# Attention by four heads at a time, values in a rotation of five PSUM banks, and a new plan of the step

## What is computed

```python
qg = split_heads(tokens @ Wqg, HEADS)          # tokens: layer norm of x
kv = split_heads(tokens @ Wkv, HEADS)
queries, gates = (qg[..., :DIM_KEYS], qg[..., DIM_KEYS:])
keys, values = (kv[..., :DIM_KEYS], kv[..., DIM_KEYS:])
queries, keys, values = (l2norm(queries), l2norm(keys), l2norm(values))
sim = jnp.einsum('bhid,bhjd->bhij', queries, keys)
attn = jnp.square(jax.nn.relu(sim))
aggr = jnp.einsum('bhij,bhjd->bhid', attn, values)
out = tanh_norm(aggr) * jnp.tanh(jax.nn.silu(gates))
x = x + out.reshape(b, n, h * d) @ Wout
...
topk_idx, topk_weight = _gate(h, gate_kernel, gate_bias)   # h: layer norm of the new x
g = jnp.einsum('nh,ehm->enm', h, w_gate)
u = jnp.einsum('nh,ehm->enm', h, w_up)
inter = jax.nn.silu(g) * u
y = jnp.einsum('ne,enh->nh', combine, jnp.einsum('enm,emh->enh', inter, w_down))
shared = jnp.dot(jax.nn.silu(jnp.dot(h, sw_gate)) * jnp.dot(h, sw_up), sw_down)
x = x + y + shared
```

## Time and profile before

| | |
|---|---|
| three runs | 689.94 us median (686.68 to 690.36) |
| profiled execution | 687.0 us, span 685.3 us |
| TensorE (PE) busy | 646.5 us, 94% of the span, 5048 matmuls |
| weight loads (PEld) | 501.7 us, 73% |
| VectorE, ScalarE, GpSimd busy | 446.9, 427.7, 420.2 us (65, 62, 61%) |
| granted TensorE clock, mean | 0.998 |
| DMA moved | 76.14 MB, queue q1 69.2% of 16 engines' span |
| L572, values on TensorE | 1024 matmuls, 145.5 us busy, 9.4 us idle before them |
| L389, squares on GpSimd | 256, 260.9 us busy, 1040 ns each |

### The profile page before, as it was taken

How to read it: one execution, slowest core, us unless ns; L and a number is a source line. 1 busy time by engine, 2 the same in 40 slices (tenths; PEclk the granted TensorE clock), 3 DMA queues, 4 the chain that set the end, 5 groups by cost and what they waited for, 6 DMA issues and landing times.

```text
span 685.3 us, 15157 instructions
## 1 busy us (share of the span) xinstructions
PE 646.5 (94%) x5048; PEld 501.7 (73%) x5048; DVE 446.9 (65%) x1701; ACT 427.7 (62%) x986; POOL 420.2 (61%) x424
## 2 busy tenths in 40 slices
PE   2788998999999999999999999999999999999877
PEld 2555566777777778777778777878778787767777
DVE  5473647676766757576676767576675766555585
ACT  3578675666677675666776675666867566544312
POOL 3157855766757576776758585776768585686300
PEclk9999999999999999999999999999999999999999
DMA  9989949496784949497694949597694939503000
GB/s 253 142 136 150 118 102 114 103 139 108 131 135 102 107 132 122 88 154 117 121 134 109 112 131 112 98 148 124 115 131 101 121 102 124 101 5 76 9 1 16
DMA packets 75517, 76.14 MB, mean 111 GB/s; under 512 B 9296, under 2 KB 73392, under 8 KB 73648
## 3 DMA queue, kind: packets, MB, share of 16 engines
q1 hardware_dynamic: 75440, 75.17, 69.2%
HBM read 56.05 MB, written 19.10 MB: 110 GB/s over the span
## 4 chain that ended last, share of the span: by engine, by line
PE 84%; DVE 5%; ACT 5%; issue 3%; POOL 2%; DMA 1%; SPq 0%; DVEq 0%; ACTq 0%; POOLq 0%
PE ps_a L572 18%; PE ps_f L421 13%; PE ps_f L422 10%; PE ps_f L423 10%; PE ps_f L488 9%; PE ps_f L512 9%; PE ps_s L540 7%; PE ps_f L463 3%; PE ps_f L484 3%; POOL p L389 2%; PE ps_f L468 1%; PE ps_f L497 1%; DMA big<-in_L_attn_Wkv 1%; ACT r L678 1%; ACT sq L638 1%
## 5 line engine op out<-in xcount | busy, mean ns | idle before, releaser
L389 POOL TENSOR_TENSOR p<-r 128x512 f32<-128x512 f32 x256 | 260.9, 1040 | 177.5 <-ACT r L678 108.9
L572 PE MATMUL ps_a<-p,v 128*64 128x256 f32 x1024 | 145.5, 394 | 9.4 <-DVE big L994 4.7
L678 ACT ACTIVATE r<-ps_s 128x512 f32<-128x512 f32 x256 | 140.7, 613 | 13.5 <-PE ps_s L540 10.6
L994 DVE TENSOR_TENSOR big<-ps_a,big 128x256 f32<-128x256 f32 x128 | 54.1, 423 | 77.8 <-ACT big L687 77.2
L572 PEld LDWEIGHTS ps_a<-p,v 128*64 128x64 f32 x1024 | 64.4, 136 | 50.1 <-DVE big L994 7.7
L670 ACT ACTIVATE it<-ps_f 128x256 f32<-128x256 f32 x144 | 56.2, 390 | 49.4 <-PE ps_f L423 41.8
L408 POOL TENSOR_TENSOR it<-it,cb 128x512 f32<-128x512 f32 x56 | 71.2, 1282 | 18.9 <-DMA cb<-c_rows 18.8
L644 ACT ACTIVATE big<-ps_f 128x512 f32<-128x512 f32 x64 | 38.2, 598 | 66.2 <-PE ps_f L423 66.2
L949 DVE TENSOR_TENSOR it<-ps_f,it 128x256 f32<-128x256 f32 x144 | 60.6, 421 | 27.7 <-ACT it L670 26.5
L512 PE MATMUL ps_f<-wdown,it 128*128 128x128 f32 x576 | 70.4, 277 | 0.8 <-DVE it L966 0.8
L512 PEld LDWEIGHTS ps_f<-wdown,it 128*128 128x128 f32 x576 | 67.6, 192 | 2.4 <-DVE it L949 1.0
(11 more groups left out here) (159 smaller groups left out, 1430.1 us busy)
## 6 DMA issues: line engine op xcount, KB each, us to landing
qk_rows<-qk_parts SPq DMA_DIRECT2D x16, 1024.0 KB, 4.8
qkt<-qk_rows SPq DMA_DIRECT2D x64, 256.0 KB, 9.9
qkt<-qk_rows SPq DMA_DIRECT2D x128, 128.0 KB, 9.0
cb<-c_rows SPq DMA_DIRECT2D x28, 512.0 KB, 6.0
x_in<-in_L_attn_tokens SPq DMA_DIRECT2D x16, 128.0 KB, 6.3
x_res<-in_L_attn_tokens SPq DMA_DIRECT2D x16, 128.0 KB, 8.7
out<-o_sb SPq DMA_DIRECT2D x16, 128.0 KB, 8.6
big<-in_L_attn_Wqg SPq DMA_DIRECT2D x1, 640.0 KB, 4.5
```

What stands on the lines that cost most here:

```text
L389: pool.tensor_tensor(p[h % 4][:], r[h % 2][:], r[h % 2][:], ALU.mult).then_inc(probs_done, 1)
L572: last = pe.matmul(ps_a[64 * e:64 * e + 64, 0:N], v[s % 3][:, t, h * DV:(h + 1) * DV], p[h % 4][:, t * N:(t + 1) * N], start=(t == 0), sto ...
L678: act.activation(r[h % 2][:], ps_s[h % 2][:], ACT.Relu).then_inc(relu_done, 1)
```

## The change

FILL is written anew, with values as a job ("A", "av", j) of its own, two at a time, in slots 1, 3, 5 and 7. The jobs use five banks ps_f0 to ps_f4 in turn; ps_a and its semaphores go. TensorE does scores j+2, values j, values j+1, scores j+3, all pairs counted on into the next step. ScalarE squares and VectorE multiplies two pairs at a time, in slots 0, 2, 4 and 6. GpSimd's and VectorE's orders are new: the routing is done in one piece in slot 0 (route_experts was in slot 2), cD comes in slot 1 (it was in slot 3), the root of L's variance in slot 3, L408 in slots 3, 5 and 7. SP's order is unchanged.

```diff
-        [("F", "lg", 0), ("P", "v", 3), ("D", "y2", 0), ("N", "ones", 0)],
-        [("N", "nT", 0), ("D", "y2", 1), ("P", "g", 0)],
-        [("F", "gu", 0), ("F", "gu", 1), ("P", "g", 1), ("F", "gu", 2)],
-        [("F", "gu", 3), ("F", "cD", 0), ("P", "g", 2), ("O", "rT", 0), ("F", "gu", 4)],
-        [("O", "rB", 0), ("O", "rB", 1), ("F", "gu", 5), ("O", "rB", 2), ("L", "xT", 0), ("O", "rB", 3), ("P", "g", 3)],
-        [("O", "y", 0), ("O", "y", 1), ("L", "qk", 0)],
-        [("F", "gu", 6), ("L", "qk", 1), ("L", "v", 0), ("F", "gu", 7)],
-        [("L", "v", 1), ("F", "gu", 8), ("O", "x2T", 0), ("L", "v", 2), SKIP, SKIP],
+        [("F", "lg", 0), ("P", "g", 0), ("D", "y2", 0), ("P", "v", 3), ("N", "ones", 0)],
+        [("D", "y2", 1), ("N", "nT", 0), ("F", "cD", 0), ("P", "g", 1), ("A", "av", 0), ("A", "av", 1)],
+        [("F", "gu", 0), ("P", "g", 2), ("F", "gu", 1), ("F", "gu", 2)],
+        [("F", "gu", 3), ("F", "gu", 4), ("F", "gu", 5), ("O", "rT", 0), SKIP, ("A", "av", 2), ("A", "av", 3)],
+        [("O", "rB", 0), ("O", "rB", 1), ("L", "xT", 0), ("O", "rB", 2), ("O", "rB", 3), ("P", "g", 3), ("L", "qk", 0)],
+        [("O", "y", 0), ("L", "qk", 1), ("L", "v", 0), ("O", "y", 1), SKIP, ("A", "av", 4), ("A", "av", 5)],
+        [("F", "gu", 6), ("L", "v", 1), ("F", "gu", 7)],
+        [("F", "gu", 8), ("O", "x2T", 0), SKIP, ("L", "v", 2), ("A", "av", 6), ("A", "av", 7)],
...
-            bank.update({job[1:]: ps_f[n % 4] for n, job in enumerate(order(s)) if job != SKIP})
+            bank.update({job[1:]: ps_f[n % 5] for n, job in enumerate(order(s)) if job != SKIP})
...
 # GpSimd, step
+                    if k == 6 and "O" in on:
+                        pool.wait_ge(ch_n, 3 * s)
+                        root(rstd2, var2, rstd2_ready)
                     if "A" in on:
                         for h in (2 * k, 2 * k + 1):
-                            wait(pool, values_done, 8 * s + (h - 4) // 2 + 1)
+                            wait(pool, done["av"], 8 * s + (h - 4) // 2 + 1)
...
-                    if k == 1 and "L" in on:
+                    if k == (1 if at == FIRST_STEP else 3) and "L" in on:
...
-                    if "P" in on and k == 4:
-                        scale_values(s + 1, 0, (0, 1))
...
-                    if "F" in on and at < B and k in (5, 6, 7):
-                        b = s - 2
-                        for j in ((0, 1), (2,), (3,))[k - 5]:
...
+                    if "P" in on and k in (4, 5):
+                        scale_values(s + 1, 0, (k - 4,))
+                    if "F" in on and at < B:
+                        for j in {3: (0, 1), 5: (2,), 7: (3,)}.get(k, ()):
+                            scale_by_combine(s - 2, j)
...
 # TensorE, step
+                            if kind == "av" and j % 2 == 0:
+                                scores_ahead(s, q, j + 2)
                             wait_for_bank(n, s, at)
                             filler(stage, kind, j, s, q, on, at)
+                            if kind == "av" and j % 2 == 1:
+                                scores_ahead(s, q, j + 2)
...
-                    if k < SLOTS - 1:
-                        if "A" in on:
-                            scores(s, q, k + 1)
-                    elif "A" in stages(at + 1):
-                        scores(s + 1, 1 - q, 0)
-                    if "A" in on:
-                        wait(pe, aw_done, 8 * s + k)
...
 # ScalarE, step
+                for k in range(SLOTS):
+                    if k % 2 == 0:
+                        relu(k)
+                        if ("A" in on and k > 0) or ("O" in on and k == 0):
+                            squared_heads(k)
+                    else:
+                        relu(k)
...
+                        if (kind, j) in gates_behind and "P" in on:
+                            gates(gates_behind[(kind, j)], s, q)
```

More of the change, by code:

```diff
@@ L73, in order @@
         return [job for slot in fill(s) for job in slot]
-    assert all(len(plan) == SLOTS and sum(len(slot) for slot in plan) % 4 == 0 for plan in (FILL, *ENDS.values()))
+    assert all(len(plan) == SLOTS and sum(len(slot) for slot in plan) % 5 == 0 for plan in (FILL, *ENDS.values()))
     OFFSET = {"L": 2, "P": 1, "N": 1, "A": 0, "O": -1, "F": -2, "D": -3}
     JOBS = {"xT": 1, "qk": 2, "v": 4, "g": 4, "ones": 1, "nT": 1, "rT": 1, "rB": 4, "y": 2,
-            "x2T": 1, "lg": 1, "gu": FC, "cD": 1, "cT": 1, "cB": 4, "y2": 2}
+            "x2T": 1, "lg": 1, "gu": FC, "av": NP, "cD": 1, "cT": 1, "cB": 4, "y2": 2}
     BY_DMA = B - 2
@@ L544, in scores, with scores_ahead, values @@
                             last.then_inc(scores_done, 1)
+            def scores_ahead(s, q, k):
+                if k < NP:
+                    scores(s, q, k)
+                elif "A" in stages(s + 1):
+                    scores(s + 1, 1 - q, k - NP)
+            def values(b, k, ps):
+                if k in (0, 4):
+                    pe.wait_ge(v_normed, 4 * b + (2 if k == 0 else 4))
+                for t in range(T):
+                    for e in range(2):
+                        h = 2 * k + e
+                        if t == 0:
+                            pe.wait_ge(probs_done, 16 * b + h + 1)
+                        last = pe.matmul(ps[64 * e:64 * e + 64, 0:N],
+                                         v[b % 3][:, t, h * DV:(h + 1) * DV], p[h % 4][:, t * N:(t + 1) * N],
+                                         start=(t == 0), stop=(t == T - 1))
+                return last
             def step(s, q, on, at):
@@ L672, in step, with relu @@
             def step(s, q, on, at):
-                for k in range(SLOTS):
+                def relu(pair):
                     if "A" in on:
-                        for h in (2 * k, 2 * k + 1):
+                        for h in (2 * pair, 2 * pair + 1):
                             wait(act, probs_done, 16 * s + h - 1)
@@ L678, in step, with squared_heads @@
                             act.activation(r[h % 2][:], ps_s[h % 2][:], ACT.Relu).then_inc(relu_done, 1)
-                    if ("A" in on and k > 0) or ("O" in on and k == 0):
-                        pair, b = (k - 1, s) if k > 0 else (NP - 1, s - 1)
+                def squared_heads(k):
+                    for i in range(2):
+                        pair, b = (k - 2 + i, s) if k > 0 else (NP - 2 + i, s - 1)
                         if pair == 0:
@@ L685, in step @@
                                 act.wait_ge(w_lo, 4)
[L686 to L687 removed]
+                        ps = (bank if k > 0 else bank_before)[("av", pair)]
+                        act.wait_ge(done["av"], NP * b + pair + 1)
+                        act.activation(a2[:, pair, :], ps[:, 0:N], ACT.Square).then_inc(a2_done, 1)
+                for k in range(SLOTS):
[5 more added lines that the diff above has]
+                        relu(k)
                     if at == -1 and k == 4:
```

147 lines of the change are left out of this document (64 added, 83 removed).

## The result

The changed kernel takes **709.32 us** (median of 4 runs, 705.82 to 714.17) beside 689.25 us of the kernel before on the same chip: a ratio of 1.031, with the 95% interval 1.0254 to 1.0365. It is 3% slower. The profiled execution took 712.05 us, its span is 710.3 us against 685.3, and 5048 matmuls are 5048 as before. The steps, from nT to nT, tell where the 25.0 us went: the first three take 3.1 us more than before, the twelve in the middle 21.9 more (mean 40.86 against 39.04), the last two 2.1 less, and 2.1 lie before the first nT and behind the last, about half in each. So it is a loss of every step with the combine weights in it.

A forecast was written before the change was run, and what follows sets the result against it. A ring from GpSimd's scaling through low_parts(1) and DMA, 40.4 us a step against 38.86, was to bound: 687.0 + 18.5 - 1.4 = 704.1, put at 705 us. Own range 697 to 712; 8 in 10, 676 to 712.

The forecast's parts named there:

- The ring: GpSimd's scaling of `it` through low_parts(1) and DMA to the next scaling: 7.4 + 33.0, 40.4 us a step (39.7 to 41.1).
- The sum: Twelve ring periods add 18.5 us, the last two steps give back 1.4: 687.0 to 704.1, forecast put at 705.
- The start: First two steps, without scaling by combine weights: TensorE waits for starts, counted as nothing, between -3 and +2 us.
- Where TensorE waits: TensorE idles 2 to 3 us a step, before values of pair 4 or 5 (GpSimd's square) and scores 6 (Relu).
- Banks: PSUM banks, every fifth job now read: found read in time, pair 3 within tenths; cost 0 to 0.3 us, taken as 0.
- What the switches save: Fewer changes of matmul form on TensorE save 1.2 us a step; TensorE alone needs 37.7, 0.4 more if score exits are free.
- Pair 3: Pair 3's values wait for gate_up(4) to free a bank: 0 to 0.3 us a step, taken as 0.
- head 15: Last head's values wait for p behind Silu, Relu and squares: about 0.5 us a step, if nothing else stops TensorE first.
- Rival 1: Small write c_rows overtakes the loads, ring 36.3 us, switches decide: 677 us, or 668 with the 0.5 hidden; chance 0.20.
- Rival 2: Emptying PSUM takes what the switches give, 1.2 us a step: about the same time, 688 us; chance 0.14.
- Rival 3: Ring binds harder: TensorE idles 2 to 3 us a step, its granted clock falls; kept inside the forecast (0.66), towards 712.
- Weight loads as the measure of TensorE: Skill's metric: weight loads 31.10 of 40, a fifth free, fewer form changes worth nothing; the prediction went by gaps instead.

The follow-up runs named there:

- experiments 1: Changed kernel with only part 0 of the scaling of `it` in GpSimd's slot 3, part 1 moved to slot 5 with part 2; 699.76 us, ratio 1.0174.
- 2: Changed kernel with parts 0, 1 and 2 of the scaling of `it` all in GpSimd's slot 3; 728.06 us, ratio 1.0576.
- experiment 3: Changed kernel with the scaling of `it` back in the slots of the kernel before (5, 6, 7); 682.1 us, ratio 0.9926.
- 10: Changed kernel with scaling in slots 4, 5, 7, first two steps' statistics earlier, and gate_up(4) ahead of value_scales; 678.03 us, ratio 0.9847.
- experiment 4: Changed kernel with the two Relus of pair 5 behind the copy and square of qk1 on ScalarE, scaling still in slot 3; 693.55 us, ratio 1.0087.
- 9: Changed kernel with only six of the twelve q and k loads from the third batch on, so the output differs; 678.64 us, ratio 0.9854.
- Experiment 12: Version 10 plus, on ScalarE, pair 7's Relus before gu 7's Silu and next batch's first Relu before v 2's copy and square; 675.73 us, ratio 0.9834.
- Experiment 8: Changed kernel with c_rows and cb issued from ScalarE's queue in place of SP's; 724.91 us, ratio 1.0553.
- experiment 5: As experiment 3, with the first two steps' layer norm sums and root two slots earlier; 679.4 us, ratio 0.9893.

## Why the prediction was right

- **The ring**, the step on which the forecast stood, held in each of its parts. L388 to the end of low_parts(1): 7.33 to 7.37 us in all twelve periods, predicted 7.4. From there to the next L388: 32.2 to 34.3, mean 33.25, predicted 33.0 and at most 33.7 on average. Ring: 40.62 by the thirteen starts of L388, predicted 40.4. It moved as it should in experiments 1 and 2, and was gone when opened at GpSimd (3, 10), in part at ScalarE (4), and at the DMA (9).
- **The sum.** Of 18.5 us for the twelve steps it was 21.9. Of the 3.4 that are missing, 2.6 is the ring's 0.22 us, twelve times over; the rest is the first of the twelve, 43.93 us beside 40.85 before. The last two steps gave back 2.1 (predicted 1.4). The start, predicted between -3 and +2, cost 3.1 in its first three steps and 1.0 before the first nT: it missed its range. Behind the last nT there is another 1.0, for which the sum has no term. The median of 709.32 is 4 us above the forecast, and that flatters the sum. The terms were added to the profiled execution, 687.0 to 704.1, and the profiled execution was 712.05: 8 us short. The medians lie closer because the forecast added 0.9 for the spread of the runs, and because this profiled execution was 2.7 above its median, which is luck.
- **Where TensorE waits.** Predicted 2 to 3 us a step before the values of pair 4 or 5, with GpSimd's square as releaser, and before scores 6. The place was right and it is 1.85 us, over the three groups of one place, a little under the forecast, in a step of 40.31; the mean ring is 0.3 longer. The releaser of the longest pause was another. Pair 5's values take the bank of qk1, five jobs back, and that is free when low_parts(1) has read it: 0.71 us [<-DVE qk_parts L846]. The point **Banks** had found all banks read in time; it looked at pair 3 and not at what the ring itself makes late. It costs little more here, as the square of head 11 ends only 0.15 us later (379.79 against 379.64).
- **What the switches save.** Predicted 1.2 us a step, TensorE alone at 37.7. Experiment 12 shows 37.76, 1.10 less than before, with 0.27 us of waiting left in the last pair's scores ahead and values (0.62 for 0.43, 1.96 for 1.88). So the switches save nearer 1.4, within the 0.4 more that I had left open for a free exit from scores. The sixteen matmuls of values took 1.88 us, predicted 1.9, with 0.31 to the scores behind, predicted 0.32.
- **Pair 3 and head 15.** gate_up(4) made pair 3 late by 0.31 us, the upper end of 0 to 0.3, where I had taken 0. Head 15 was predicted at 0.5: its values wait 0.39, the scores ahead of it 0.16 and behind it 0.09, together 0.64. All of it is invisible in the changed kernel's time, since the ring sets its step, and shows once the ring is open (38.41 in experiment 3).
- **Rival 1** fell, but my reason for it fell too. c_rows was issued 18.8 us after low_parts(1) (I said 18) and took 6.7 us, until the loads had drained. I leaned on the order within one queue (the Trainium skill, "DMA: Bandwidth & Descriptors", section Queues, rings and completion order). Experiment 8 puts the write on a queue of its own, and it still lands 0.3 to 1.7 us after the last load. The rule isn't refuted; it isn't what decides here. The price of this rival with the 0.5 hidden, 668, was also summed wrongly: 14 steps of 1.2 from 687.0 give 670.
- **Rival 2**, at 688 us, needed the ring open. Opened, the waits for other engines took 0.65 us of 1.10 (38.41 against 37.76), not all, and changes of order on VectorE, ScalarE and GpSimd gave it back. Not all of that is emptying PSUM: GpSimd's scaling ahead of the last squares is a part.
- **Rival 3** did not come: TensorE waited for the ring in every step, yet its granted clock stayed at 1.00 from 137.3 to 622.0 us. In experiments 2 and 8, whose steps are longer (up to 44.0 and 44.3 us), it did fall to 0.50 again and again.
- **Weight loads as the measure of TensorE** (the Trainium skill, "Trainium Kernel Development and Optimization", section Performance Expectations). By it TensorE has a fifth of its time free, here too (31.38 of 40). I read into it that fewer changes of form would be worth nothing, but the section only speaks of how close a kernel is to roofline. Taking away changes of form and waits cut the step from 38.86 to 37.76, with weight loads at 32.17 of 40 in experiment 12. What could be gained, and where, the gaps told.

What stays open is the start. In every version with the new order the first two steps take 52.0 to 53.8 us together (56.7 in experiment 4), beside 48.6 before. Between 20 and 48 us the granted clock was 0.83 in the changed kernel and 1.00 before, and between 20 and 80 us TensorE waited 5.4 us for squares of v (L656; 3.1 before) and 4.6 us for normalized rows (none before). Which of these leads I did not find out; experiment 5 shows that earlier statistics alone don't mend it.

## What to carry to other kernels

Before a wait is moved up an in-order queue, list what comes to stand behind it and follow that until it meets what the wait is for: if it does, the step can't be shorter than the sum once around, however free each engine looks. The bounding engine hides such a ring while it is longer than the ring, so the place of the wait matters more than its length; in experiments 4 and 10 GpSimd kept waiting and the steady steps lost little or nothing. And a busy TensorE is measured by the distance of its groups in two versions laid side by side, which found 1.85 of 1.90 us in one place.

## What was not expected of the hardware

A write of 16 KB, alone on its queue q10, took 5.8 us (median) and landed 0.3 to 1.7 us after the last load on q1. That is no better than behind them on q1 itself, where it landed 0.4 to 1.8 us after the last load (7.2 us after its issue, which came earlier against the loads). Where no loads were under way it took 2.3 us, and 1.9 (median) with half the loads, which had landed before its issue in every step but the first. Here a queue of its own bought a small transfer no way past the 2 MB of loads of a step.
